# Row tiles moved as two pieces instead of three, and nine units of edge work placed earlier in the last layer

## What is computed

```python
def _mgcn_conv(x, edge_index, edge_type, rel, W_in, W_out, W_loop, b, n):
    m = x[src] * rel[edge_type]
    m = jnp.concatenate([m[:half] @ W_in, m[half:] @ W_out], 0)
    agg = jax.ops.segment_sum(m * norm[dst][:, None], dst, num_segments=n)
    return jnp.tanh(agg + x @ W_loop + b)
...
h = emb + res * _mgcn_conv(emb, ..., rel1, ...)        # graph layer 1
h = h + res * _mgcn_conv(h, ..., rel2, ...)            # graph layer 2
gnn = h @ mu_w + mu_b
...
for i in range(4):                                     # the mixing branch
    x = x + _linear_attn(_layernorm(x), ...)
    x = x + gelu(_layernorm(x) @ W1[i] + b1[i]) @ W2[i] + b2[i]
...
x = x + gnn + mix
x = x + shared_mlp(ln(x)) + top2_of_4_experts(ln(x))
```

## Time and profile before

| | us |
|---|---|
| median of 3 runs | 1943.16 |
| lowest and highest | 1937.86, 1951.39 |
| profiled execution | 1951.01 |
| its span, first to last instruction | 1949.2 |

### The profile page before, as it was taken

How to read it: one execution, slowest core, us unless ns; L and a number is a source line. 1 busy time by engine, 2 the same in 40 slices (tenths; PEclk the granted TensorE clock), 3 DMA queues, 4 the chain that set the end, 5 groups by cost and what they waited for, 6 DMA issues and landing times. The chain is left out here.

```text
span 1949.2 us, 28362 instructions
## 1 busy us (share of the span) xinstructions
PE 1757.6 (90%) x9423; PEld 1294.2 (66%) x9423; DVE 1223.5 (63%) x3583; ACT 628.7 (32%) x1552; POOL 1300.5 (67%) x1297
## 2 busy tenths in 40 slices
PE   2788999998899999989999978987998998988998
PEld 1355867776587777758777645655776676766787
DVE  6777455664756576575556464487665666478766
ACT  4442233343233434333333332231221222222333
POOL 6776777777777777777777733755777676666300
PEclk9999999999899999999999999999999999999999
DMA  9667666667766666776666764667867565555301
GB/s 250 196 200 234 195 207 192 200 191 224 245 197 207 204 193 202 220 248 196 192 203 209 210 192 127 188 197 215 241 192 214 183 202 184 167 176 179 108 14 27
DMA packets 195923, 371.44 MB, mean 191 GB/s; under 512 B 39343, under 2 KB 127445, under 8 KB 195780
## 3 DMA queue, kind: packets, MB, share of 16 engines
q0 software_dynamic: 74304, 220.71, 39.0%
q1 hardware_dynamic: 93124, 126.68, 20.2%
q10 hardware_dynamic: 28352, 22.24, 4.2%
HBM read 305.39 MB, written 64.95 MB: 190 GB/s over the span
## 5 line engine op out<-in xcount | busy, mean ns | idle before, releaser
L1049 POOL DMA_INDIRECT xg<-h_rows,idx_tab x416 | 426.8, 1026 | 205.9 <-issue 125.1
L1049 POOL DMA_INDIRECT xg<-xn_rows,idx_tab x416 | 432.7, 1040 | 141.6 <-issue 123.4
L1001 POOL DMA_INDIRECT rg<-relation_rows,idx_tab x416 | 417.2, 1003 | 136.4 <-issue 126.2
L2880 PE MATMUL ps_hid<-hT,wff 128*128 128x250 f32 (+1 forms) x1920 | 372.3, 347 | 7.0 <-ACT gT L2314 7.0
L2892 PE MATMUL ps_down<-wff,gT 128*125 128x256 f32 x1600 | 366.1, 382 | 0.0
L2880 PEld LDWEIGHTS ps_hid<-hT,wff 128*128 128x128 f32 x1920 | 313.7, 192 | 59.1 <-issue 27.0
L1144 DVE TENSOR_TENSOR xg<-xg,rg 128x256 f32<-128x256 f32 x832 | 296.6, 418 | 71.4 <-DMA xg<-h_rows,idx_tab 40.1
L2892 PEld LDWEIGHTS ps_down<-wff,gT 128*125 128x125 f32 x1600 | 295.4, 189 | 46.3 <-issue 5.1
L2751 PE MATMUL ps_seg<-xg,hot 128*61 128x257 f32 (+1 forms) x1664 | 233.9, 404 | 39.3 <-DVE xg L1144 34.3
L2314 ACT ACTIVATE gT<-ps_hid,b1p 128x250 f32<-128x250 f32 (+1 forms) x480 | 176.8, 434 | 286.6 <-PE ps_hid L2880 286.4
L2751 PEld LDWEIGHTS ps_seg<-xg,hot 128*61 128x61 f32 (+1 forms) x1664 | 103.1, 139 | 134.6 <-issue 67.3
(11 more groups left out here) (382 smaller groups left out, 2420.5 us busy)
## 6 DMA issues: line engine op xcount, KB each, us to landing
second_relation_rows<-rg SPq DMA_DIRECT2D x104, 512.0 KB, 4.0
rg<-second_relation_rows SPq DMA_DIRECT2D x104, 512.0 KB, 4.0
wff<-L_mix_W ACTq DMA_DIRECT2D x8, 1024.0 KB, 7.2
rg<-relation_rows,idx_tab POOLq DMA_INDIRECT x416
xg<-xn_rows,idx_tab POOLq DMA_INDIRECT x416
xg<-h_rows,idx_tab POOLq DMA_INDIRECT x416
h_rows<-qT_all SPq DMA_DIRECT2D x25, 64.0 KB
qrow<-h_rows ACTq DMA_DIRECT2D x25, 64.0 KB
```

What stands on the lines that cost most here:

```text
L1001: pool.indirect_dma_start(rg[:, k, :], None, rel_d, indices(step, 1)).then_inc(s_edge[k // UNIT], 16)
L1049: pool.indirect_dma_start(xg[:, k, 0:D], None, rows, indices(step, 0)).then_inc(s_edge[k // UNIT], 16)
L2880: ins = pe.matmul(hidden, w1[:, c, ff * P:(ff + 1) * P], hT[:, a:z, c, :], start=c == 0, stop=c == KC - 1)
```

## The change

The moves of single tiles use the two strips as their pieces, 64 and 61 rows; the moves of groups keep the three pieces. The semaphore counts that wait for tiles follow.

Of the edge steps, 36 (nine units, all of graph layer 2) leave the last part: one unit goes to group 4 of layer 2, three to the joint of layer 3, two to group 0 of layer 3, one each to its groups 2, 3 and 4. The last part keeps 64 steps, 16 units. The flush of the last sums into `acc` there is tied to the step at which PE is through with the units.

```diff
-STEPS_JOINT = (16, 16, 16, 20)
-STEPS_GROUP = ((16, 24, 24, 24, 24), (16, 24, 24, 24, 24), (16, 24, 24, 48, 52), (36, 40, 56, 56, 56))
-STEPS_LAST = 100
+STEPS_JOINT = (16, 16, 16, 32)
+STEPS_GROUP = ((16, 24, 24, 24, 24), (16, 24, 24, 24, 24), (16, 24, 24, 48, 56), (44, 40, 60, 60, 60))
+STEPS_LAST = 64
...
     PIECES = ((0, 64), (64, CUT), (CUT, T))
+    TILE_PIECES = STRIPS
...
-        s_h1 = [counted(f"h1_stored{k}", 16 * len(PIECES)) for k in range(SLOTS)]
+        s_h1 = [counted(f"h1_stored{k}", 16 * len(TILE_PIECES)) for k in range(SLOTS)]
...
         def move_tile(eng, rows, dram, t, done, store=False):
-            for a, z in PIECES:
+            for a, z in TILE_PIECES:
                 ends = rows[a:z], tile_rows(dram, t, a, z)
                 eng.dma_start(*(ends[::-1] if store else ends)).then_inc(done, 16)
...
-            sp.wait_ge(s_out, MOVED * (NG - 1 + GT))
+            sp.wait_ge(s_out, MOVED * (NG - 1) + TILE_MOVED * GT)
...
                 upto(last_units(s, 1))
-                if edges.done == UNITS and edges.adds < ADDS:
+                if last_units(s, 1) == STEPS_LAST // UNIT and edges.adds < ADDS:
                     edges.flush()
```

More of the change, by code:

```diff
@@ L626, in build @@
         MOVED = 16 * len(PIECES)
+        TILE_MOVED = 16 * len(TILE_PIECES)
         def rows_of(w):
@@ L914, in _ @@
             for k in range(SLOTS):
-                sp.wait_ge(s_h1[k], MOVED * (len(range(k, NT, SLOTS)) + 1))
+                sp.wait_ge(s_h1[k], TILE_MOVED * (len(range(k, NT, SLOTS)) + 1))
             def load_relations(u):
@@ L1038, in _ @@
                     for k in range(SLOTS):
-                        pool.wait_ge(s_h1[k], MOVED * (len(range(k, NT, SLOTS)) + 1))
+                        pool.wait_ge(s_h1[k], TILE_MOVED * (len(range(k, NT, SLOTS)) + 1))
                 for step in range(STEPS2):
@@ L1828, in dense_tile @@
                     dve.wait_ge(s_dy, i + 3)
-                    dve.wait_ge(s_h1[t % SLOTS], MOVED * (t // SLOTS) + MOVED)
+                    dve.wait_ge(s_h1[t % SLOTS], TILE_MOVED * (t // SLOTS) + TILE_MOVED)
                     dve.tensor_tensor(h_new[t % SLOTS], ps_dense[i % 2][0:T, 0:D], bias_of(t), ALU.add).then_inc(s_db, 1)
@@ L2473, in joint @@
                     for k in range(SLOTS):
-                        act.wait_ge(s_h1[k], MOVED * (len(range(k, NT, SLOTS)) + 1))
+                        act.wait_ge(s_h1[k], TILE_MOVED * (len(range(k, NT, SLOTS)) + 1))
                     for t in range(GT):
@@ L3225, in turn_sums @@
                         h = t % AHEAD
-                        pe.wait_ge(s_hx[h], (t - h) // AHEAD * MOVED + MOVED)
+                        pe.wait_ge(s_hx[h], (t - h) // AHEAD * TILE_MOVED + TILE_MOVED)
                         turned = transpose_rows(pe, ps_sums[i % 2][:, KC * T:2 * KC * T], h_rows[h])
@@ L3269, in turn_sums @@
                     h = t % GT
-                    pe.wait_ge(s_hx[h], (dense_loads(h) + t // GT + 1) * MOVED)
+                    pe.wait_ge(s_hx[h], (dense_loads(h) + t // GT + 1) * TILE_MOVED)
                     turned = transpose_rows(pe, ps_x2[:, KC * T:2 * KC * T], qrow[:, h, :])
```

## The result

| | before | after |
|---|---|---|
| median, us | 1944.07 (4 runs) | 2047.96 (4 runs) |
| lowest to highest | 1937.86 to 1951.39 | 2046.3 to 2049.06 |
| span of the profiled execution | 1949.2 | 2047.2 |

The account below looks back on a forecast made before the run. PE paces most stretches, SP's issuing and the store-to-store loop the dense one. Dense stretch +57, output +2, ACT's loads +1 and units -2 give +58 on 1943, said as 2000 us; range 1962 to 2035.

Parts of the forecast that it names:

- SP's issuing and the loop from store to store pace the stretch before: Dense stretch, 1113 to 1203 us: SP's three issues take 1.53 us; DVE waits 28.8 us for stores.
- 61 rows lie on one engine: Single-tile moves: a 61-row piece runs on one DMA engine at 22 GB/s, 2.84 us each, 6.06 us a turn.
- The dense stretch, +57: Layer 2's dense stretch: one engine's queued loads, stores and gathers lengthen its 90 us by 51 to 64, taken as +57.
- The last output +2: End of the kernel: the last tile's output saves an issue of 0.4 us, but its last rows take 2.84 us: +2 us.
- six loads ahead 0: Six loads issued before the dense stretch put 18 us on one engine, a group piece earlier; costed at nothing.
- ACT's loads in layer 3, +1 (0 to +8): ACT's 25 loads in layer 3 and the last part: 2.84 us more each, hidden by five tiles' distance; +1 us.
- The nine units, -2 (-15 to +15): Nine units moved out of the last part: -18 us there, +6 in layer 3's joint, +10 in groups; -2 us.
- The +16 for what comes in: Moved units' cost: three in layer 3's joint at 2 us each, +6; six in groups at 1.7 each, +10.
- Rival 3: POOL doesn't keep up in layer 3: units cost 5.3 us instead of 1.7, 2020 us; chance 0.11.
- Rival 4: Each of 25 bursts on one engine makes a gather wait 2.84 us, half reaching PE: 2035 us; chance 0.07.
- Rival 2: Dense stretch: loads and stores overlap on the one engine, 3 us a turn, +30 there, 1973 us; chance 0.13.
- Rival 1: The 61 rows spread over engines like 48 and 13; dense stretch loses 17 us, 1924 us; chance 0.08.

Follow-up runs that it names:

- 60 and 1: Single-tile moves in three pieces of 64, 60 and 1 rows, edge steps as before, against the kernel before: 1940.7 us, ratio 0.9953.
- 60 against 59 rows: Single-tile pieces of 64, 60 and 1 rows against 64, 59 and 2, both with the edge steps of before: 1940.7 us against 2023.4 us.
- The slowed POOL: Kernel before, with four small memsets on POOL behind each unit's gathers in groups 2, 3 and 4 of layer 3: 1984.7 us, ratio 1.0189.
- a unit less: On pieces of 64, 60 and 1 rows, four units moved from layer 2's group 4 and layer 3's groups 2 to 4 into the last part: 1949.6 us.

## Why the prediction was wrong

- **SP's issuing and the loop from store to store pace the stretch before:** shown. 0.14 us less for three issues (60 and 1), 6 us in all, shortened it by some 7 us; two pieces made DVE's wait 88.6 us, where about 80 were foreseen.
- **61 rows lie on one engine:** shown, by 60 against 59 rows and by the flat 24 GB/s. The engine's rate was put at 22 GB/s, so that a turn came to 6.06 us; at 24 it measured 5.53.
- **The dense stretch, +57:** right. The turns came 6.5 us apart over the first 19 (1113.7 to 1237.0 us), 5.5 without a relation store; the stretch was 147 us long, and POOL's first gather of graph layer 2 ended at 1260.7 us, 56.9 later than before. The total fits better than its parts: the first 19 turns took 123 us where the sum has 123 to 136, the rest 24 where it has 18.
- **The last output +2, six loads ahead 0:** the last issue starts at 2042.2 us and the span ends 5.0 us later, against 1.8 before: +3. No place was found for the six loads.
- **ACT's loads in layer 3, +1 (0 to +8):** here a step failed. It said that the engine's extra work is hidden by the distance of five tiles, and that ACT's issuing is no bound because ACT is busy for 75 of 343 us. Both hold for the data, not for the issue: an issue behind two unfinished pieces of 61 rows does not return in half a microsecond, and ten of them stood ahead of the one GELU that PE needed. A sign of it stood in the earlier trace rows: two issues took 0.61 us, and the one of a single row behind the 103 rows took 2.03. +19.5 us alone, and 20.7 taken back by three pieces there. The prediction costed these loads by their bytes, 71 us of one engine; what counted was the time for which they held the engine that issues them.
- **The nine units, -2 (-15 to +15):** here the second step failed, in the size of a term. -18 for the last part measured -15.6. The +16 for what comes in measured +39: the five units in joint and group 0 cost 11.9 us where 9.4 stood, and the four groups with one unit each grew by 27.1 us where 6.8 stood, 6 to 8 us a unit instead of 1.7. The prediction took POOL's ring wait of 33.5 us as room for five more units. Little of it is room: POOL waits at the turn of the groups (6.1, 7.3 and 7.8 us from 1528.9, 1610.9 and 1691.3 us on) and is behind at other places, as DVE's 29.3 us for gathers said in the same rows. The slowed POOL shows it: 52 us more brought 39.
- **Rival 3**, POOL too slow for the added units: not shown as their price. It gave 5.3 us a unit, and 6 to 8 were measured; with the units alone DVE's wait for gathers grew by 1.9 us only and POOL's ring wait by 8; and a unit less brought 3 us at most. What grew with the units are the waits of PE and DVE for each other, PE's for `xres` from 11.1 to 20.8 us. How much of a unit's price is POOL's and how much the order of units in the lists of DVE and PE stays open.
- **Rival 4**, gathers held up behind bursts on the one engine: not shown at any size that matters; with the pieces alone DVE's wait for gathers in groups 2 to 4 is 29.8 us against 24.6. **Rival 2**, loads and stores side by side: refuted by the turn of 5.5 us (its own sum comes to 1974 us, not 1973). **Rival 1** fell with 60 against 59 rows.

The direction and the largest term were right. 2000 + 18 for ACT's loads + 25 for the units is 2043, against 2048. Each of the two misses alone would have stayed within the range; together they left it.

What stays open: what makes a unit cost 6 to 8 us in a group, and the last part's price at 29 units. A load of 64 rows for the second strip too, two issues with a row count like the first strip's, would need rows past the strip's end and was not tried.

## What to carry to other kernels

Before two DMAs are made one, factor the row count: here 61 rows in one piece lost 50 us in the dense stretch against 48 and 13, and 60 and 1 gained 0.5% in all. DMAs that lie on one engine are not costed by bytes alone: look at which instruction stands behind their issue on the issuing engine, and who waits for that. And a wait at a ring is not slack as it stands: POOL, with 21 us of ring waits in three groups, took up some 13 of 52 us of added work and passed on 39.

## What was not expected of the hardware

An issue on ACT's or SP's queue took some 0.45 us with nothing ahead of it, and up to 6.1 us on ACT and 3.8 us on SP behind unfinished pieces of 61 rows; I read that as held until the one engine has room. One engine alone moved rows of 1 KB at 42.5 ns each, loads and stores one after the other. A gather kept POOL almost as long for 16 rows (0.92 us in the mean) as for 128 (1.01).
